# One decoder kernel: a norm between statistics and second softmax, sums behind the former norm, a reordered head, and semaphores cleared without a barrier

## The chip, the cores and the metric

The kernel runs on one core of a Trainium2 chip. The metric is the device time of one execution in microseconds (us). The core has five engines that run their own instruction queues in order and meet through semaphores: PE (TensorE, matrix products; its weight loads are listed as PEld), DVE (VectorE), ACT (ScalarE), POOL (GpSimd) and SP (SyncE, which here only issues DMAs).

## The reference, cut to what matters

The reference is a two-layer decoder over 64 sequences of 64 rows with 128 numbers each, all in float32. Six blocks follow one another, each added to the residual `x`:

```
x = x + L0_attn(layernorm(x))            # linear attention and a soft mixture of 4 experts
x = x + L0_xattn(ctx, layernorm(x))      # latent attention
x = x + L0_ffn(layernorm(x))             # shared MLP and 2 of 8 routed experts
x = x + L1_attn(layernorm(x))            # causal attention, below
x = x + L1_xattn(layernorm(x), ctx, mask)# attention with a relative bias
x = x + L1_ffn(layernorm(x))             # top expert of 8

# L1_attn, 16 heads of 8 numbers
q, k, v = heads(x @ Wq + bq), heads(x @ Wk + bk), heads(x @ Wv + bv)
att = softmax(where(causal, q @ k.T / sqrt(8), -inf))
y = (att @ v) @ Wo + bo
```

The change touches the border between the second and the third block, and the fourth block, the causal attention.

## The kernel before, in words

The whole residual `X` (32 tiles of 128 rows by 128) stays in SBUF. The six blocks are stages in one program: linear attention, latent attention, routing with the shared MLP (`route_and_share`), the routed experts (`run_experts`), causal attention (`causal_attention`), biased attention, top expert. Each stage is one block of code for each engine, and a barrier of all engines stands at the end of every block: an engine that is through waits until the last one is. Nothing but this barrier and the semaphores orders the engines. The order on each engine is written out by hand.

**The border of latent attention and routing.** Semaphores are scarce, so `reuse_semaphores` (lines 59 to 63) lets GpSimd clear the ones of the first two stages (L61), frees them, and puts a second barrier of all engines (L63) behind the one of the block's end. Only then do the engines enter `route_and_share`. PE begins there with L1279, DVE with the statistics of the last two tiles (L142 and after), GpSimd with a memset (L1331) and a root (L155).

**Causal attention** works in 16 steps of two tiles (256 rows, 4 sequences). For step s the work goes through these hands:

- SP gathers the two expert results of each row (L1825). GpSimd weighs them, adds the pair and adds this to `X` (L2153, L2158, L2164: "the sums" of a step, function `combine`).
- DVE takes the statistics of the rows (`norm_stats`, L142 to L149), GpSimd the inverse root (`norm_root`, L155), DVE applies the norm and writes `ca_xn` (`norm_apply`, L162).
- PE transposes `ca_xn` (L1901), ACT copies it out as `ca_hT` (L2058), PE projects q and k (L1909), ACT spreads them (L2063 and L2068), PE computes masked scores in two halves (L1933 adds the mask, L1938 the products).
- For each half DVE takes the maximum (L2231) and subtracts it (L2234), ACT takes the exponential (L2089), PE transposes (L1948), ACT copies (L2084), PE multiplies with v and the ones (L1965). DVE takes the reciprocal and the product of the step (`normalise`, L2239 and L2241), PE projects (L1977, L1979), DVE adds to `X` (`add`, L2246).

The steps are interleaved by `run_steps`, LEAD 3 and DEPTH 4: bodies 0, 1 and 2 are written out, 3 to 10 run in a loop of two bodies, 11 to 16 are written out again. Body s on DVE does, in order: first softmax of step s, statistics of step s+2, `add` of step s-2, second softmax of step s, norm of step s+2, `normalise` of step s-1. (Bodies 0 and 1 have their norm ahead of the second softmax.) Body s on PE does: first scores of s, transposes of the second half of s-1, `project` of s-2, the other transposes of s-1 and its first products, q and k projections of s+1 (between them a wait for the first softmax of s), second scores of s, v projection, transposes of the first half of s, the second products of s-1, then a wait for the second softmax of s, and last `turn_rows` of step s+2 (L1901), which waits for the norm of s+2.

GpSimd does, step after step, the sums and the root; for steps 1 to 3 it waits for the norm of the step before ahead of its sums, and for later steps it does not.

**The head of the stage** (before body 0) also computes keys and values of the next stage's first step: on PE `next_context`, four `next_keys` (L1851), `turn_rows` and `project_qk` of step 0, then `next_values` 4 and 5 (L1870, two passes for each); values 6 and 7 follow in body 0. ACT copies each of them (L2093).

**Late in the stage** SP waits for the sums of step 15 and then stores the relative bias in 254 KB of short rows and loads it back (L1831, L1836).

## Time and profile before

| | us |
|---|---|
| median of 3 runs (1894.44 to 1898.54) | 1895.55 |
| the profiled execution: its time | 1896.96 |
| the profiled execution: its span, first to last instruction | 1894.8 |
| PE busy | 1811.2 (96% of the span) |
| DVE busy | 1241.3 (66%) |
| ACT busy | 883.9 (47%) |
| POOL busy | 630.0 (33%) |
| mean granted clock of PE, 1 is full speed | 0.990 |

The stages stand at these places: linear attention to 414 us, latent attention to 955, routing and shared MLP to 1136, experts to 1247, causal attention to 1451, biased attention to about 1827, top expert to the end. The profiled execution took 1.41 us more than the median of the runs, and 2.16 us of its time lie outside its span. The page also gives the clock that PE was granted; it is at full speed nearly everywhere and at half in a few stretches of some us.

### The profile page before, as it was taken

Reading aid. Unit: us, or ns where it says so; the run is one execution under the profiler, and the core shown is the slowest. Engines: PE = TensorE matmul, PEld = TensorE weight load, DVE = VectorE, ACT = ScalarE, POOL = GpSimd, SP = SyncE. Lnnn points to the kernel's source line nnn. Section 1 sums busy time; section 2 is a strip of 40 time slices with the busy share of each in tenths; the row PEclk is TensorE's granted clock in tenths of the full one; section 3 lists DMA queues with packets and bytes.
Section 4 is the critical chain, followed back from the end, with each engine's and each line's share of the span. In section 5 each row is a group of like instructions: output and inputs, shape, how many; then the busy total and the mean of one; then the engine's idle time right before and its main releaser. Section 6 shows DMA issues by size and latency. Waiting matters only on the chain. (4 is left out here: it accounts for less than half of the span.)

```text
span 1894.8 us, 49825 instructions
## 1 busy us (share of the span) xinstructions
PE 1811.2 (96%) x20072; PEld 1353.8 (71%) x20072; DVE 1241.3 (66%) x2986; ACT 883.9 (47%) x1694; POOL 630.0 (33%) x744
## 2 busy tenths in 40 slices
PE   7999999999999999999999999989988999999978
PEld 5566666667888888888756667857766788888743
DVE  6677777647667766666643322237877888888877
ACT  1444444455555555555432213347664444445435
POOL 2111111113333333333314533342221444444547
PEclk9999999999999999999999999989999999999999
DMA  9200000000000000000010002210010000000001
GB/s 326 82 2 0 0 0 0 1 1 1 1 1 0 0 0 0 0 0 0 1 78 28 29 23 94 96 54 25 28 36 3 2 3 2 3 2 3 2 7 40
DMA packets 37926, 46.16 MB, mean 24 GB/s; under 512 B 5000, under 2 KB 32443, under 8 KB 37266
## 3 DMA queue, kind: packets, MB, share of 16 engines
q1 hardware_dynamic: 34450, 38.43, 6.5%
q0 software_dynamic: 3328, 5.58, 0.9%
q8 instruction: 115, 1.88, 0.4%
q14 instruction: 33, 0.27, 0.0%
HBM read 28.67 MB, written 17.10 MB: 24 GB/s over the span
## 5 line engine op out<-in xcount | busy, mean ns | idle before, releaser
L155 POOL TENSOR_TENSOR rstd<-var_eps,minus_half 128x2 f32<-128x2 f32 (+1 forms) x116 | 92.1, 794 | 466.6 <-DVE var_eps L149 466.4
L1069 POOL TENSOR_TENSOR xa_probs<-xa_probs,xa_total 128x512 f32<-128x512 f32 x128 | 133.0, 1039 | 196.4 <-DVE xa_total L1110 191.7
L1115 DVE TENSOR_REDUCE xa_top<-ps 128x4 f32<-128x512 f32 x128 | 88.1, 688 | 128.0 <-PE ps L934 126.7
L1030 ACT ACTIVATE xa_probs<-xa_probs 128x512 f32<-128x512 f32 x128 | 80.8, 631 | 157.4 <-DVE xa_probs L1118 157.4
L923 PEld LDWEIGHTS ps<-xa_kvT,pack_latent 128*128 128x128 f32 x512 | 96.6, 190 | 65.7 <-issue 43.7
L934 PE MATMUL ps<-xa_kvT,xa_qT 128*128 128x128 f32 x1024 | 135.3, 275 | 0.0
L950 PE MATMUL ps<-xa_probsT,xa_kv 128*128 128x512 f32 x256 | 133.2, 602 | 1.9 <-ACT xa_attnT L1039 1.8
L396 PEld LDWEIGHTS ps<-pack_moe,la_hid 128*128 128x128 f32 x1024 | 121.0, 192 | 17.4 <-issue 15.3
L383 PE MATMUL ps<-la_h2T,pack_moe 128*128 128x512 f32 x256 | 128.3, 609 | 3.9 <-ACT la_hid L592 3.9
L923 PE MATMUL ps<-xa_kvT,pack_latent 128*128 128x256 f32 x512 | 130.6, 380 | 1.4 <-PEq L344 1.4
L396 PE MATMUL ps<-pack_moe,la_hid 128*128 128x128 f32 x1024 | 125.2, 277 | 0.0
L934 PEld LDWEIGHTS ps<-xa_kvT,xa_qT 128*128 128x128 f32 x1024 | 124.5, 192 | 0.1
L592 ACT ACTIVATE la_hid<-ps,pack_moe 128x512 f32<-128x512 f32 x128 | 86.9, 686 | 80.2 <-PE ps L383 78.4
L958 PEld LDWEIGHTS ps<-pack_latent,xa_attnT 128*128 128x128 f32 x1024 | 118.2, 192 | 3.3 <-issue 2.5
L958 PE MATMUL ps<-pack_latent,xa_attnT 128*128 128x128 f32 x1024 | 119.6, 275 | 0.8 <-ACT xa_attnT L1039 0.8
L2416 PE MATMUL ps<-ba_inT,pack_latent 128*64 128x128 f32 x1920 | 118.1, 277 | 1.2 <-DVEq L1813 1.2
L2597 POOL TENSOR_TENSOR ba_probs<-ba_probs,ba_bias 128x512 f32<-128x512 f32 x64 | 81.4, 1272 | 101.1 <-DVE ba_probs L2662 101.1
L1463 DVE TENSOR_TENSOR rt_mid<-ps,rt_silu 128x512 f32<-128x512 f32 x64 | 44.2, 691 | 106.6 <-ACT rt_silu L1317 106.6
L1027 ACT ACTIVATE xa_probsT<-ps 128x512 f32<-128x512 f32 x128 | 76.8, 600 | 75.5 <-PE ps L943 75.5
L2416 PEld LDWEIGHTS ps<-ba_inT,pack_latent 128*64 128x64 f32 x1920 | 103.7, 137 | 8.0 <-issue 1.4
L1108 DVE TENSOR_REDUCE xa_total<-xa_probs 128x4 f32<-128x512 f32 x128 | 87.3, 682 | 22.2 <-ACT xa_probs L1030 21.6
L1118 DVE TENSOR_TENSOR xa_probs<-ps,xa_top 128x512 f32<-128x512 f32 x128 | 88.6, 692 | 13.0
(357 smaller groups left out, 4034.5 us busy)
## 6 DMA issues: line engine op xcount, KB each, us to landing
expert_weights<-experts_dram SPq DMA_DIRECT2D x8, 768.0 KB, 5.3
result_pairs<-zeros SPq DMA_DIRECT2D x1, 4096.0 KB, 30.9
ca_got<-result_pairs SPq DMA_DIRECT2D x16, 256.0 KB, 2.6
slot_rows<-zeros SPq DMA_DIRECT2D x1, 2880.0 KB, 19.7
expert_rows<-slot_rows SPq DMA_DIRECT2D x8, 360.0 KB, 3.1
pack_moe<-moe_dram SPq DMA_DIRECT2D x1, 2312.0 KB
pack_latent<-latent_dram SPq DMA_DIRECT2D x1, 2050.0 KB, 14.1
pack_latent<-biased_dram SPq DMA_DIRECT2D x1, 2048.0 KB, 8.0
```

What stands on the lines that cost most here:

```text
L155: pool.tensor_tensor(m.rstd[:, 0:tiles], m.var_eps[:, 0:tiles], m.minus_half[:, 0:tiles], ALU.pow).then_inc(sem.rstd, 1)
L383: pe.matmul(HIDDEN[n % 2], w["w1"][:, n // F0, n % F0, :], h2T[:], start=True, stop=True)\
L396: mm = pe.matmul(out, hid[:, n % 2, f, P * t:P * t + P], w["w2"][:, n, f, :], start=(f == 0), stop=(f == F0 - 1))
L923: mm = pe.matmul(bank(PROJ_BANK + n % 2)[:, NS * a:NS * a + NS], qk_fold[:, 2 * n + a, :], kvT[:, k, :, SEQ:], start=True, stop=True)
L934: mm = pe.matmul(bank(u % 2)[:, KEYS * n:KEYS * n + KEYS], qT[:, k, seq, head:head + 2, :].rearrange("p a q -> p (a q)"), kvT[:, k, seq, : ...
L950: pe.matmul(bank(ATTN_BANK), kv[:, k, seq, :], probsT[:, u % 2, :], start=True, stop=True)\
L958: mm = pe.matmul(bank(OUT_BANK)[:, P * t:P * t + P], attnT[:, t, h, :], vo_fold[:, h, :], start=(h == 0), stop=(h == H - 1))
L1069: pool.tensor_tensor(probs[:, u % 4], probs[:, u % 4], over(total[:, u % 4], 2, KEYS), ALU.mult).then_inc(probs_ready, 1)
L1108: dve.tensor_reduce(total[:, u % 4], probs[:, u % 4], AX.X, ALU.add).then_inc(sum_ready, 1)
L1115: dve.tensor_reduce(top[:, s % 4], scores, AX.X, ALU.max).then_inc(top_ready, 1)
L1118: dve.tensor_tensor(probs[:, s % 4], scores, over(top[:, s % 4], 2, KEYS), ALU.subtract)\
L2416: mm = pe.matmul(proj_bank(n)[SEQ * seq:SEQ * seq + SEQ, P * h:P * h + P], (w["bq"], w["bk"])[n // 4][:, at:at + DHX], tokens[:, seq], sta ...
```

## The change

In four parts:

1. `reuse_semaphores` is gone. The list of old semaphores is handed down (`past_semaphores`), the new stage takes fresh ones, and GpSimd clears the old ones at the start of `route_and_share`, between the barrier at the end of latent attention and its own first instruction. No second barrier follows.
2. On DVE the norm of step s+2 moves from behind the second softmax of step s to ahead of it, behind `add`, for bodies 2 to 13. Body 1 keeps its order (its norm stood ahead already). In body 0 the order is now softmax, statistics of step 2, softmax, norm of step 2, statistics of step 3; before, the statistics of step 2 stood ahead of the first softmax and the norm between the two.
3. On GpSimd the sums of every step from 4 on wait for the norm of the step before. The sums of step 3 are done right behind those of step 2, ahead of the root of step 2.
4. In the head, PE does `next_values(4)` ahead of `turn_rows` of step 0, ACT copies it ahead of the step's own copies, and ACT copies the context for the keys one instruction earlier (0.27 us between the two starts before).

```diff
-def reuse_semaphores(nc, m):
-
-    nc.clear_and_free_semaphores(m.stage_semaphores)
-    m.stage_semaphores = []
-    nc.all_engine_barrier()
+def past_semaphores(m):
+
+    past, m.stage_semaphores = m.stage_semaphores, []
+    return past
...
+        nc.clear_and_free_semaphores(past)
         with nc.Block() as block:
...
                 for n in range(4):
                     next_keys(n)
+                next_values(4)
                 turn_rows(step_of(0, 0), 0)
                 project_qk(step_of(0, 0), 0, None)
-                next_values(4)
                 next_values(5)
...
+                act.wait_ge(ctx_turned, 1)
+                act.activation(biased.inT[:, 1, :], bank(QK_BANK)[:, 0:NS], ACT.Copy).then_inc(ctx_ready, 1)
                 act.wait_ge(out_bias_done, 1)
                 act.wait_ge(zeroed, 2)
                 act.activation(tiles_of(out_bias[0:1, :]), over(bank(1)[0:1, 0:D], 1, 2), ACT.Copy).then_inc(out_bias_ready, 1)
-                act.wait_ge(ctx_turned, 1)
-                act.activation(biased.inT[:, 1, :], bank(QK_BANK)[:, 0:NS], ACT.Copy).then_inc(ctx_ready, 1)
                 for n in range(4):
                     copy_next_kv(n)
+                copy_next_kv(4)
                 rows(step_of(0, 0), 0)
                 copies_q(step_of(0, 0), 0)
                 copies_k(step_of(0, 0), 0)
-                copy_next_kv(4)
                 copy_next_kv(5)
...
-                for step in range(STEPS):
-                    if 1 <= step <= SETS:
-                        pool.wait_ge(ln.normed, 2 * step)
+                for step in range(2):
+                    combine(step)
+                    root(step)
+                    pool.wait_ge(ln.normed, 2 * step + 2)
+                combine(2)
+                combine(3)
+                root(2)
+                root(3)
+                for step in range(4, STEPS):
+                    pool.wait_ge(ln.normed, 2 * step)
                     combine(step)
                     root(step)
...
                         softmax(step, 0)
                     if ahead >= 2 and has(step, 2):
                         stats(later(step, 2))
-                    if ahead >= 2 and not has(step, 2):
-                        normed(later(step, 2))
+                    if not before:
+                        stats(later(step, 2))
                     if ahead == 0:
                         scale_mask()
                     if has(step, 2):
                         add(later(step, -2))
+                    if ahead >= 2 and before:
+                        normed(later(step, 2))
                     if here:
                         softmax(step, 1)
                     if not before:
+                        normed(later(step, 2))
                         stats(later(step, 3))
-                    if ahead >= 2 and has(step, 2):
-                        normed(later(step, 2))
...
-                stats(step_of(0, 2))
                 run_steps(dve, STEPS, body, DEPTH, LEAD)
...
-        reuse_semaphores(nc, m)
-        routed_experts(nc, m)
+        routed_experts(nc, m, past_semaphores(m))
```

What stands where is easiest seen in the order of the instructions. DVE in body 2, from `add` of step 0 on (`ca_top` and `ca_probs` are the second softmax of step 2, `ca_xn` the norm of step 4, `ca_rden` and `ca_attnT` belong to `normalise`), before:

```order
L2246 TENSOR_TENSOR X<-ps,X 128x256
L2231 TENSOR_REDUCE ca_top<-ps 128x16
L2234 TENSOR_TENSOR ca_probs<-ps,ca_top 128x1024
L162 TENSOR_SCALAR ca_xn<-X,mean_var,rstd 128x128 x2
L2239 RECIPROCAL ca_rden<-ps 128x256
L2241 TENSOR_TENSOR ca_attnT<-ps,ca_rden 128x256
```

The same place on DVE in the changed kernel:

```order
L2253 TENSOR_TENSOR X<-ps,X 128x256
L161 TENSOR_SCALAR ca_xn<-X,mean_var,rstd 128x128 x2
L2238 TENSOR_REDUCE ca_top<-ps 128x16
L2241 TENSOR_TENSOR ca_probs<-ps,ca_top 128x1024
L2246 RECIPROCAL ca_rden<-ps 128x256
L2248 TENSOR_TENSOR ca_attnT<-ps,ca_rden 128x256
```

The norm has moved from behind the second softmax to ahead of it; the reciprocal now follows the softmax at once.

POOL from the root of step 1 on to the root of step 3 (`ca_got` and `X` are the sums), before:

```order
L155 TENSOR_TENSOR rstd<-var_eps,minus_half 128x2
L2153 TENSOR_TENSOR ca_got<-ca_got,pair_weights 128x512
L2158 TENSOR_TENSOR ca_got<-ca_got 128x2x128
L2164 TENSOR_TENSOR X<-X,ca_got 128x256
L155 TENSOR_TENSOR rstd<-var_eps,minus_half 128x2
L2153 TENSOR_TENSOR ca_got<-ca_got,pair_weights 128x512
L2158 TENSOR_TENSOR ca_got<-ca_got 128x2x128
L2164 TENSOR_TENSOR X<-X,ca_got 128x256
L155 TENSOR_TENSOR rstd<-var_eps,minus_half 128x2
```

The same place on POOL in the changed kernel, behind the root of step 1:

```order
L2153 TENSOR_TENSOR ca_got<-ca_got,pair_weights 128x512
L2158 TENSOR_TENSOR ca_got<-ca_got 128x2x128
L2164 TENSOR_TENSOR X<-X,ca_got 128x256
L2153 TENSOR_TENSOR ca_got<-ca_got,pair_weights 128x512
L2158 TENSOR_TENSOR ca_got<-ca_got 128x2x128
L2164 TENSOR_TENSOR X<-X,ca_got 128x256
L154 TENSOR_TENSOR rstd<-var_eps,minus_half 128x2 x2
```

The sums of step 3 stand ahead of the root of step 2. The order of the later steps is as before; what is new there is the wait ahead of the sums.

PE in the head of the stage, from the keys on to the first scores (`ca_xn` and `ca_hT` belong to step 0; `pack_latent` with `ba_inT` are `next_values`), before:

```order
L1851 MATMUL ps<-ba_inT,pack_latent 64x128 x32
L1901 MATMUL ps<-pack_constants,ca_xn 128x128 x2
L1909 MATMUL ps<-ca_hT,pack_causal 128x256 x2
L1870 MATMUL ps<-pack_latent,ba_inT 128x512 x2
L1933 MATMUL ps<-pack_later_constants,pack_constants 32x256 x16
```

The same place on PE in the changed kernel:

```order
L1851 MATMUL ps<-ba_inT,pack_latent 64x128 x32
L1870 MATMUL ps<-pack_latent,ba_inT 128x512
L1901 MATMUL ps<-pack_constants,ca_xn 128x128 x2
L1909 MATMUL ps<-ca_hT,pack_causal 128x256 x2
L1870 MATMUL ps<-pack_latent,ba_inT 128x512
L1933 MATMUL ps<-pack_later_constants,pack_constants 32x256 x16
```

One of the two value products now stands ahead of the transposes of step 0.

## Rows read from the trace of the kernel before

**Rows 1.** Waits, 1290 to 1400 us: who waited for whom, us in total, times, longest.

```profile
DVE ca_top L2231 <- PE ps L1938: 15.0, 11, 1.6
...
PE ps L1901 <- DVE ca_xn L162: 4.5, 10, 0.6
```

**Rows 2.** Waits of PE, 1400 to 1430 us.

```profile
PE ps L1901 <- DVE ca_xn L162: 0.6, 1, 0.6
```

**Rows 3.** Timeline of one loop step: start, length, engine, work, [idle before <- releaser].

```profile
1325.44 1.23 DVE L2231 TENSOR_REDUCE ca_top<-ps 128x16 f32<-128x1024 f32 x1 [1.25 <-PE ps L1938]
...
1327.91 0.60 DVE L162 TENSOR_SCALAR ca_xn<-X,mean_var,rstd 128x128 f32 x2
...
1328.42 1.75 DVE L2239 RECIPROCAL ca_rden<-ps 128x256 f32<-128x256 f32 x1
...
1328.64 0.43 PE L1901 MATMUL ps<-pack_constants,ca_xn 128*128 128x128 f32 x2 [0.43 <-DVE ca_xn L162]
1328.74 1.05 ACT L2089 ACTIVATE ca_probs<-ca_probs 128x1024 f32<-128x1024 f32 x1
...
1330.32 0.66 PE L1948 MATMUL ps<-pack_constants,ca_probs 128*128 128x128 f32 x4
1330.55 1.21 DVE L2231 TENSOR_REDUCE ca_top<-ps 128x16 f32<-128x1024 f32 x1
...
1334.05 0.71 POOL L155 TENSOR_TENSOR rstd<-var_eps,minus_half 128x2 f32<-128x2 f32 x1 [6.92 <-DVE var_eps L149]
...
1334.73 1.05 POOL L2153 TENSOR_TENSOR ca_got<-ca_got,pair_weights 128x512 f32<-128x512 f32 x1
...
1335.80 1.23 DVE L2231 TENSOR_REDUCE ca_top<-ps 128x16 f32<-128x1024 f32 x1 [1.32 <-PE ps L1938]
...
1336.67 0.73 POOL L2164 TENSOR_TENSOR X<-X,ca_got 128x256 f32<-128x256 f32 x1
```

**Rows 4.** Timeline of DVE, second softmax of step 1 and of step 2.

```profile
1284.26 1.23 DVE L2231 TENSOR_REDUCE ca_top<-ps 128x16 f32<-128x1024 f32 x1 [3.19 <-PE ps L1938]
...
1294.20 1.22 DVE L2231 TENSOR_REDUCE ca_top<-ps 128x16 f32<-128x1024 f32 x1 [1.60 <-PE ps L1938]
```

**Rows 5.** Timeline, end of latent attention and start of routing: two barriers between.

```profile
954.62 0.42 DVE L1123 TENSOR_TENSOR X<-ps,X 128x256 f32<-128x256 f32 x1 [11.07 <-PE ps L958]
...
956.64 1.10 PE L1279 MATMUL ps<-turned_rows,pack_shared 128*128 128x512 f32 x2 [2.05 <-PEq L63]
```

**Rows 6.** Timeline, end of routing and start of the experts: one barrier between.

```profile
1134.85 0.69 DVE L1469 TENSOR_TENSOR X<-ps,X 128x512 f32<-128x512 f32 x1 [7.50 <-PE ps L1289]
...
1136.08 0.73 PE L1579 MATMUL ps<-pack_constants,expert_rows 128*128 128x128 f32 x5 [1.26 <-PEq L1226]
```

**Rows 7.** Waits of SP's queue, 940 to 965 us.

```profile
SPq L63 <- PEq L63: 1.0, 1, 1.0
```

**Rows 8.** Timeline of the causal stage's head.

```profile
1260.48 0.69 PE L1901 MATMUL ps<-pack_constants,ca_xn 128*128 128x128 f32 x2 [2.79 <-DVE ca_xn L162]
...
1263.51 3.60 PE L1870 MATMUL ps<-pack_latent,ba_inT 128*128 128x512 f32 x4
...
1264.66 1.02 ACT L2068 ACTIVATE ca_kpairs<-ps,ca_kbias,pack_constants 128x256 f32<-128x256 f32 x2
...
1267.03 0.71 PE L1933 MATMUL ps<-pack_later_constants,pack_constants 32*32 32x256 f32 x32
...
1268.35 1.98 PE L1870 MATMUL ps<-pack_latent,ba_inT 128*128 128x512 f32 x4
```

**Rows 9.** Windows: stretch, length, busy us of PE, PEld, DVE, ACT, POOL, clock, DMA, GB/s.

```profile
1266.00:1268.00 2.00, 2.00 (x42) 0.56 (x44) 0.00 (x0) 0.77 (x2) 1.84 (x3) 0.76 0.00 0
```

**Rows 10.** Timeline of SP and PE late in the stage.

```profile
1399.84 5.46 SPq L1831 DMA_DIRECT2D skewed_bias<-ca_by_offset  x2
...
1413.03 1.33 SPq L1836 DMA_DIRECT2D bias_values<-skewed_bias  x2
...
1414.82 0.54 PE L1965 MATMUL ps<-ca_probsT,ca_vheads 128*32 128x64 f32 x11 [4.20 <-issue]
```

More of the change, by code:

```diff
@@ L1132, in _, with routed_experts @@
                 dve.wait_ge(noted, 2 * (STEPS - 1))
-def routed_experts(nc, m):
+def routed_experts(nc, m, past):
     with ExitStack() as ctx:
@@ L1143, in routed_experts @@
         m.expert_loaded = [stage_semaphore(nc, m, "expert_loaded_" + name) for name in ("even", "odd")]
-        route_and_share(nc, m)
+        route_and_share(nc, m, past)
         run_experts(nc, m)
@@ L1154, in load_weights, with route_and_share @@
         .then_inc(m.expert_loaded[k], 16)
-def route_and_share(nc, m):
+def route_and_share(nc, m, past):
     w = m.w
```

## The prediction

> **What bounds the kernel now.** The page says that PE is busy for 96% of the span, so I asked in each stretch that the change touches what PE still waits for. In the table of waits of the causal loop PE has one wait worth naming: its transposes of a step's rows (L1901) wait for the norm on DVE, 4.5 us in 10 times [rows 1]. An eleventh, 0.6 us, stands behind it [rows 2], just ahead of a stall of 4.2 us in the middle of PE's products (L1965) that is put down to "issue", PE's own instruction supply [rows 10]. DVE waits for PE in the same loop, 15.0 us in 11 times [rows 1]: neither engine is full, they wait for each other in turn, and what decides is the order on DVE. The timeline of one step shows it [rows 3]. The second softmax starts at 1325.44, and from there to 1335.80 is one step, 10.36 us. The norm comes behind it at 1327.91, PE takes it at 1328.64 after 0.43 us of idling. But the root that this norm needs was ready a whole half step earlier: in the step that follows, the root ends at 1334.05 + 0.71 = 1334.76, and then DVE idles until 1335.80 (1.32 us of idle time before the softmax). The norm stands on the wrong side of a hole.
>
> **The loop: the norm into the hole.** The norm is two instructions, 0.60 us together. Put behind the root it runs from about 1334.85 to 1335.45, and the softmax is not due before 1335.80: it is hidden by DVE's wait for the scores, with 0.35 us to spare. Behind the softmax the reciprocal moves up from 1328.42 to 1327.91, so the next first softmax can start at 1330.55 - 0.51 = 1330.04 instead of 1330.55; PE's scores, moved up by its own wait of 0.43, ask for it at about 1330.0. Both engines move by nearly the same, so the step should shrink by PE's wait. Eleven such waits are 4.5 + 0.6 = 5.1 us. **Minus 5.1.** One step of the old trace already looks like this: in body 1 the norm stood ahead of the second softmax, PE did not wait, and from its second softmax to the next one are 1294.20 - 1284.26 = 9.94 us [rows 4], 0.42 less than 10.36.
>
> What is late next is ACT. PE's transposes at 1330.32 need the exponential that runs from 1328.74 to 1329.79 [rows 3]; moved up by 0.43 they stand at 1329.89, 0.10 behind it. So 0.43 is nearly all that there is to have, and at worst some of it is lost.
>
> **The loop: the sums behind the norm.** GpSimd now waits for the norm before the sums of the next step. In the old step's times they start at about 1335.5 instead of 1334.73, 0.75 later, and end 0.75 later. Behind the waiting instruction stand the sums and the next root. The statistics that read the sums come most of a step later: GpSimd sat idle for 6.92 us ahead of its root [rows 3]. Cost on the path: nothing, with 6 us of cover. The gathers that wait for a slot are three steps ahead.
>
> On why the wait is there: in the trace the softmax's maximum takes 1.23 us with sums beside it and 1.21 without them [rows 3], so these two do not disturb each other; a norm beside sums is not in these rows. The Trainium skill (SBUF — State Buffer, "Who interferes with whom") says that a tensor_scalar from SBUF to SBUF can need the port pair that DVE shares with GpSimd, and that the second to come is blocked for a whole instruction of the other. By that rule sums let go straight behind the root would hold the norm in the hole. The wait excludes this, so the sum above is the same with the rule and without it; the rule only gives the slow rival below its mechanism.
>
> **The late sums' other customer.** SP stores the relative bias when the sums of step 15 are done. These also come 0.75 us later against PE. The store was issued at 1399.84, the load that waits for its landing at 1413.03 [rows 10], and PE's stall, from 1410.6 on, ends at 1414.82, between 1 and 2 us behind that. I read the stall as PE's next piece of code being fetched behind the store's many short rows. If so, its end moves with the store: the stall grows by the same 0.75. Bounds: 0 (its end hangs on something else that moves with PE) and +0.75. I take the upper end, since the stall ends so near to the store's landing. **Plus 0.75.**
>
> **The border.** With two barriers PE starts 956.64 - (954.62 + 0.42) = 1.60 us after DVE's last instruction [rows 5]; at the next border, with one, it is 1136.08 - (1134.85 + 0.69) = 0.54 us [rows 6]. The difference is 1.06; SP's queue waits 1.0 us for the second barrier [rows 7]. The clearing itself stays on GpSimd alone. Its first result that anyone needs is the root behind DVE's statistics, about 1 us into the stage, so it has cover for that long, and any excess would delay only DVE's small norm, not PE's first products. Bounds 0.8 and 1.06. **Minus 1.0**, since the stage is PE-bound from its first instruction and everything behind moves up with it, the gathers included.
>
> **The head.** PE idles 2.79 us for the norm of step 0 (L1901 at 1260.48), and later does four passes of two value products at 1263.51 in 3.60 us, ahead of the first scores at 1267.03 [rows 8]. One product now falls into the idle time, which costs nothing there, and 1.8 us go from in front of the scores. But the scores also need ACT's spread keys, ready at 1264.66 + 1.02 = 1265.68. So they start at about 1265.74, 1.29 earlier. Of this some goes again: those four passes took 3.60 us where the same four took 1.98 a little later [rows 8], because PE's clock is at half speed there until about 1267 (mean 0.76 over the window from 1266 [rows 9]). Scores that start earlier run in the slow stretch: the 1.32 us from 1267.03 to 1268.35 become up to twice as long until 1267, so the values behind them start at about 1267.5 instead of 1268.35. Bounds 0 (DVE or ACT next late) and 1.29; I take 0.8. DVE's new order in body 0 has the first softmax no longer behind statistics, so it can follow. **Minus 0.8.** The keys that start 0.27 earlier end in the idle time: nothing.
>
> **The sum.** -1.0 - 5.1 + 0.75 - 0.8 = -6.15 us. The profiled execution, 1896.96, would become 1890.8, with a span of 1888.65; it lies 1.41 above the median of the runs. From the median: 1895.55 - 6.15 = **1889.4 us**, 0.32% faster.
>
> **The rivals.**
> A. The clock stays up in the head. PE idled 2.79 us and found half speed; with a value product in it the idle time is about 1.9, and the fall may not come. Then the chain from 1260.48 to the scores runs at full speed: the four passes show 1.98 against 3.60 [rows 8], and at this rate the two projections save 0.9 too. The scores come at about 1264.5 and the values behind them at 1265.8, 2.55 earlier than before instead of 0.8: 1887.7. For it: the idle time is shorter. Against it: still the longest of the head. The Trainium skill (TensorE: Matmul & The Clock Gate, "What's actually happening") says that the monitor runs free of the kernel, so by it this could differ from run to run; no run here shows that yet.
> B. The DVE wait goes and another takes half of its place, ACT's exponential first of all (0.10 of cover). Then the loop gives 2.5 instead of 5.1: 1892.0. Against it: the 9.94 of body 1. For it: body 1 has no statistics and no `add`.
> C. The store gets out of the way: if PE's fetch is asked for before the store begins, 0.75 later is enough to let it pass, and the 4.2 us go, with the 0.75. 1889.4 - 4.95 = 1884.5. For this the fetch would have to be asked for within that 0.75 us, of a step of some 10.
> D. Slower: the sums come ahead of the norm on the shared port, or the wait holds the wrong side. The three sums last 1336.67 + 0.73 - 1334.73 = 2.67 us [rows 3]. A norm behind them ends at about 1337.5 + 0.6 = 1338.1 instead of 1335.45; with 0.35 of cover the second softmax is 2.3 late in every step: 9.93 + 2.3 = 12.2 against 10.36, 1.9 us in each of 11 steps, +21 instead of -5.1: about 1915. It decides from 0.35 + 0.43 = 0.78 us of delay of the norm on. Against it: the norm needs the root alone, and the wait keeps the sums behind it.
> That the change doesn't do what it says is excluded: the order of the instructions shows all four parts.
>
> **How the numbers follow.** Chances: the forecast 0.52 (1887.5 to 1891), A 0.17, B 0.17, C 0.06, D 0.04, and 0.04 for a mean clock that is worse elsewhere by one or two slow stretches (up to 3 us, 1892.5). A measurement of this kernel can tell about 0.2%, 3.8 us, from no change: faster is below 1891.8. The forecast, A, C and nearly half of B are faster (0.81 together, 0.78 with the spread of the runs, which is 4 us); the rest of B and the bad clock are the same, 0.17; slower 0.05. The range runs from 1886.5 (A and its spread) to 1892.5 (B), which leaves out C, D and the tails.
>
> **What would show each step.** No wait of L1901 for `ca_xn` in the loop, and a step of about 9.93 from second softmax to second softmax; the norm in DVE's hole, 0.1 behind the root; the stall at L1965 near 4.95 with the store's issue 0.75 nearer to it; 0.5 to 0.8 us between DVE's last instruction and PE's first at the border; one value product in PE's idle time and the first scores 1.3 earlier against the norm of step 0. The prediction is wrong if the step stays above 10.1, if the stall changes by more than 1 us, or if the stage behind takes back what this one gives.

## The result, and the profile after

| | before | after |
|---|---|---|
| median of 4 runs each, us | 1897.05 | 1885.68 |
| lowest to highest | 1894.44 to 1898.68 | 1881.68 to 1886.33 |
| profiled execution, span | 1894.8 | 1884.4 |

The ratio is 0.9943, with a 95% interval of 0.992 to 0.9965. The forecast was 1889.4 us, with a range of 1886.5 to 1892.5: the direction was right, and the time lies below the range. Two more measurements of the changed kernel, in later groups of runs, gave 0.9965 [0.9943, 0.9987] and 0.9951 [0.993, 0.9971]. The plain mean of the three is 0.9953, some 8.9 us. The median of the kernel before was itself 1893.4 to 1896.9 us in the larger groups (11 to 31 runs each), so the starting point of the forecast, 1895.55 from 3 runs, was only good to 2 us.

Read one profile against the other, stretch by stretch. The border first, in the timeline of the changed kernel (start, length, engine, work, idle time before and its releaser):

```profile
954.80 0.42 DVE L1122 TENSOR_TENSOR X<-ps,X 128x256 f32<-128x256 f32 x1 [11.07 <-PE ps L957]
...
955.76 1.10 PE L1279 MATMUL ps<-turned_rows,pack_shared 128*128 128x512 f32 x2 [1.00 <-PEq L896]
...
956.53 0.12 POOL L1331 MEMSET rt_half_power<- 128x32 f32 x1 [6.37 <-remote]
...
956.82 0.70 POOL L154 TENSOR_TENSOR rstd<-var_eps,minus_half 128x2 f32<-128x2 f32 x1 [0.16 <-DVE var_eps L148]
```

From DVE's last instruction to PE's first are now 955.76 - 955.22 = 0.54 us, against 1.60 in [rows 5]: 1.06 us less, as at the other border [rows 6]. The clearing holds GpSimd back to 956.53, 0.77 us behind PE's first product, and its root follows DVE's statistics by 0.16 us.

The loop, with the same two views as [rows 1] and [rows 3]. The waits, 1290 to 1400 us (PE has none left in this view):

```profile
DVE ca_top L2238 <- PE ps L1938: 5.3, 12, 0.5
DVE ca_xn L161 <- POOL rstd L154: 4.9, 11, 0.6
```

One step of the timeline:

```profile
1324.98 1.23 DVE L2238 TENSOR_REDUCE ca_top<-ps 128x16 f32<-128x1024 f32 x1 [0.46 <-PE ps L1938]
...
1327.75 0.43 PE L1901 MATMUL ps<-pack_constants,ca_xn 128*128 128x128 f32 x2
...
1333.08 0.71 POOL L154 TENSOR_TENSOR rstd<-var_eps,minus_half 128x2 f32<-128x2 f32 x1 [5.81 <-DVE var_eps L148]
...
1333.82 0.60 DVE L161 TENSOR_SCALAR ca_xn<-X,mean_var,rstd 128x128 f32 x2 [0.44 <-POOL rstd L154]
...
1334.50 1.05 POOL L2153 TENSOR_TENSOR ca_got<-ca_got,pair_weights 128x512 f32<-128x512 f32 x1 [0.72 <-DVE ca_xn L161]
...
1334.91 1.23 DVE L2238 TENSOR_REDUCE ca_top<-ps 128x16 f32<-128x1024 f32 x1 [0.49 <-PE ps L1938]
```

The norm stands in DVE's hole, 0.03 us behind the root. It is done 0.49 us before the softmax, the sums start 0.08 us behind it, and PE's transposes at 1327.75 wait for nothing. The step is 9.93 us, and PE has no gap in it.

The end of the stage is the place where the two profiles differ most. The marks are the second softmax of step 12 and the first of step 15. (The rows stored and loaded back in between are two stores of 254 KB each.) Before:

```profile
1398.30 1.23 DVE L2231 TENSOR_REDUCE ca_top<-ps 128x16 f32<-128x1024 f32 x1 [1.64 <-PE ps L1938]
...
1432.55 1.22 DVE L2231 TENSOR_REDUCE ca_top<-ps 128x16 f32<-128x1024 f32 x1
```

After:

```profile
1395.10 1.23 DVE L2238 TENSOR_REDUCE ca_top<-ps 128x16 f32<-128x1024 f32 x1 [0.43 <-PE ps L1938]
...
1397.52 4.88 SPq L1831 DMA_DIRECT2D skewed_bias<-ca_by_offset  x2
...
1410.86 1.33 SPq L1836 DMA_DIRECT2D bias_values<-skewed_bias  x2
...
1422.01 1.22 DVE L2238 TENSOR_REDUCE ca_top<-ps 128x16 f32<-128x1024 f32 x1
```

The stretch takes 34.25 us before and 26.91 after. PE's stall of 4.20 us [rows 10] is gone, and with it a stretch at half speed behind it. In windows (length, busy us of PE, PEld, DVE, ACT, POOL, clock, DMA share, GB/s), before from 1415:

```profile
1415.00:1420.00 5.00, 5.00 (x85) 3.46 (x82) 2.49 (x3) 1.81 (x3) 0.00 (x0) 0.50 0.68 197
```

and the changed kernel from 1405 to 1418, where the stores' rows and then the loads run:

```profile
1405.00:1418.00 13.00, 13.00 (x373) 9.97 (x388) 10.13 (x12) 9.55 (x23) 0.00 (x0) 1.00 0.46 105
```

The head is the last of the four parts. The changed kernel:

```profile
1262.68 0.44 PE L1901 MATMUL ps<-pack_constants,ca_xn 128*128 128x128 f32 x2 [3.04 <-DVE ca_xn L161]
...
1267.78 0.73 PE L1933 MATMUL ps<-pack_later_constants,pack_constants 32*32 32x256 f32 x32 [0.77 <-ACT ca_kpairs L2068]
...
1294.95 1.22 DVE L2238 TENSOR_REDUCE ca_top<-ps 128x16 f32<-128x1024 f32 x1 [0.43 <-PE ps L1938]
```

From PE's first transposes (L1901) to the second softmax of step 2 are 32.27 us, against 1294.20 - 1260.48 = 33.72 in [rows 4, 8]. Summed over the profile: up to the second softmax of step 2 +0.75 us (border and head gained, and a slow stretch at the start of the experts took more: mean clock 0.79 from 1134 to 1142, where it was 1.00 before); from there to the second softmax of step 12 100.15 instead of 104.10, -3.95; from there to the first of step 15 -7.34; behind it nothing more. That is 10.5 us, and 7.3 of it in a stretch that took 34. The pair is a favourable one: the same stretch took 33.2 to 34.3 us in the other profiles with a stall of 4.2 us or a little less, and 27.8 and 28.0 in two more profiles of the changed kernel.

### The profile page after: what moved, and what is told of

Its sections match the earlier page's. It is cut to its first block and busy times, and to the rows that moved or that the text cites. A ratio compares the mean times of both kernels' runs of the same rounds, so it can differ in the third digit from the quotient of the medians.

```text
span 1884.4 us, 49825 instructions
## 1 busy us (share of the span) xinstructions
PE 1810.4 (96%) x20072; PEld 1351.4 (72%) x20072; DVE 1241.9 (66%) x2986; ACT 884.4 (47%) x1694; POOL 631.5 (34%) x744
```

## The experiments

Three questions: is the loop's gain what the forecast says, what does GpSimd's wait do, and is the stall, which the forecast let grow by 0.75 us, where the extra gain is from. All ratios are to the kernel before, in the same group of runs.

**The two kernels again.** No edit.

> The kernel before, unchanged, for a second trace. Theory 1 (PE's stall of 4.2 us late in the causal stage is a piece of PE's code that queues behind the store of the relative bias, at a place set by the kernel): the stall is there again, 3.5 to 5 us, at the same matmul line, and the half-speed stretch behind it too. Theory 2 (the stall is an accident of one execution): it is absent or elsewhere. The expert stage, first copy of turned rows to the causal stage's first copy, took 113.6 us in the old trace and 116.8 in the new one: if that is an accident of the execution, it may come out anywhere between here.

One run, 1897.79 us; the stall 3.94 us, and the waits of L1901 as before.

> The changed kernel, unchanged, for a second trace and its ratio on this chip: 0.992 to 0.9965. Theory 1: no stall of PE above 1 us inside the last written-out bodies, again. Theory 2: the stall may be back. Loop step 9.95 to 10.05 us.

0.9965 [0.9943, 0.9987], span 1884.4. The loop is the same to 0.1 us, and PE's stall is 0.63:

```profile
1407.46 0.36 PE L1965 MATMUL ps<-ca_probsT,ca_vheads 128*32 128x64 f32 x10 [0.63 <-issue]
```

**The parts alone.** The border (the clearing on GpSimd, no barrier):

```
-        reuse_semaphores(nc, m)
-        routed_experts(nc, m)
+        routed_experts(nc, m, past_semaphores(m))
```

> The kernel before with the clearing moved into the stage and no second barrier, nothing else. From the rows of the border: minus 1.06 us, ratio 0.9994, the stall of 4.2 us unchanged. If the clearing moves more than the border (fresh semaphores, shifted code), the stall or the expert stage differs.

0.9986 [0.9971, 1.0001]. Its profile repeats the 0.53 us between DVE and PE; a gain of 1 us is inside the interval, and no more can be said. The stall (4.19) and the expert stage are as before.

The head (value product 4 and its copy ahead of the projections, the context copied first; the edit on PE is shown):

```
+                next_values(4)
                 turn_rows(step_of(0, 0), 0)
                 project_qk(step_of(0, 0), 0, None)
-                next_values(4)
```

> The kernel before with the reordered head alone: value product 4 ahead of the transposes of step 0, context copied first. My own sum said 1.3 us less from the norm of step 0 to the first scores, of which 0.8 stays up to the later steps; full speed of PE in that stretch would give up to 2.5. In the changed kernel 1.45 us (first trace) and 0.3 us (second trace) came out from norm 0 to the second softmax of step 2, with the statistics moved as well. Rival: the statistics of step 2 ahead of the first softmax hold it, so the head alone gives less than 0.5.

0.9998 [0.9984, 1.0013]. Its profile, from the first transposes on:

```profile
1262.59 0.44 PE L1901 MATMUL ps<-pack_constants,ca_xn 128*128 128x128 f32 x2 [2.20 <-DVE ca_xn L162]
...
1266.75 0.73 PE L1933 MATMUL ps<-pack_later_constants,pack_constants 32*32 32x256 f32 x32 [1.26 <-ACT ca_kpairs L2068]
...
1273.97 0.70 PE L1909 MATMUL ps<-ca_hT,pack_causal 128*128 128x256 f32 x2 [2.27 <-DVE ca_probs L2234]
```

and its windows (columns as above, the clock third from the end):

```profile
1270.00:1275.00 5.00, 1.99 (x39) 0.85 (x37) 3.76 (x10) 3.20 (x5) 1.73 (x3) 1.00 0.17 52
1275.00:1280.00 5.00, 4.31 (x82) 3.08 (x56) 3.18 (x8) 3.11 (x10) 2.02 (x3) 0.66 0.20 56
```

The clock stays up from 1262 to 1269 (mean 1.00; 0.51 from 1260 to 1267 before), and the scores come 4.16 us behind the transposes instead of 6.55. Then PE waits 2.27 us for DVE, which in the old order has statistics ahead of its first softmax, and goes to half speed behind that. The second softmax of step 2 comes 35.00 us behind the transposes, not 33.72.

This can't be put down to the moved product. The unedited head shows the same in another execution, that of the kernel before with its stores early (below): scores 4.15 us behind the transposes, the clock up, and then

```profile
1275.89 0.70 PE L1910 MATMUL ps<-ca_hT,pack_causal 128*128 128x256 f32 x2 [2.25 <-DVE ca_probs L2235]
```

with its second softmax of step 2 at 34.92 us; the second trace of the kernel before has 34.96. In the twelve profiles with DVE's old order in body 0 this stretch takes 33.5 to 35.0 us (mean 34.2), and the first softmax of step 0 stands 8.8 to 8.9 us behind the transposes in all of them, whether the scores come at 4.2 or at 6.6. So the reorder alone shows no gain, and what the first steps wait for is DVE.

The loop (DVE's order and GpSimd's waits, border and head as before):

> The kernel before with the change's loop alone: DVE's order of norm, statistics and softmax, and GpSimd's waits; border and head as before. Theory (the loop gives what the forecast gave it, 4.5 to 5.1 us, in every execution, and the stall at L1965 weighs little in most timed ones): step 10.04 us, no wait of L1901 for ca_xn, 5 to 6 us off in the median, a ratio of 0.997. Rival (the stall is in every execution, so the loop part, which moves the stores, brings its 6 to 7 us too): 11 us or more off, a ratio of 0.994. If the extra 1.7 to 3.2 us of the expert stage in the profiles of the changed kernel come from the loop's code, the time from the stage's start to the causal stage is 115.3 us here too, and 113.6 us otherwise.

0.9958 [0.9938, 0.9977], in 6 runs. From the first transposes to the second softmax of step 2 are 1294.90 - 1262.35 = 32.55 us here. In the eight profiles with DVE's new order this stretch takes 31.3 to 33.5 us (mean 32.4), and the first softmax stands 5.6 to 6.8 us behind the transposes. So a gain of the head's size is there with DVE's new order in the first bodies alone, with PE idle for 3.49 us ahead of the transposes and no product moved.

The expert stage has the slow stretch at its start here too (0.79 from 1134 to 1142; 1.00 in the kernel with the border alone), as in the profile of the changed kernel. It stands in seven of the eight profiles with the new order and in none of the other twelve, and from the first expert product to the transposes of step 0 the eight take 125.3 to 127.5 us, the twelve 124.2 to 125.0. The difference of the means, 1.6 us, takes back nearly all of the 1.8 us that the stretch behind it gains. Why code that runs 120 us later should do this, no run tells.

**The norm in the hole without GpSimd's wait.** DVE's order alone, on the kernel before:

```
                     if has(step, 2):
                         add(later(step, -2))
+                    if ahead >= 2 and has(step, 2):
+                        normed(later(step, 2))
                     if here:
                         softmax(step, 1)
                     if not before:
                         stats(later(step, 3))
-                    if ahead >= 2 and has(step, 2):
-                        normed(later(step, 2))
```

(for the first two bodies the order stays as it was)

> The kernel before with the norm ahead of the second softmax from body 2 on, nothing else: GpSimd's sums start straight behind the root, beside the norm. Theory of the loop: PE's wait of 0.43 goes in 11 steps, minus 4.5 to 5.1 us there. If sums and norm disturb each other, the norm takes 1 us or more instead of 0.60 and the step stays at 10.3 or grows. Stall theory 1: the store's issue stays 1.5 us behind the second softmax of step 12 or comes earlier against it, so the stall of 4.2 us stays; if it goes, the shorter step alone is enough.

1.001 [0.9989, 1.0031]: no gain at all. The timeline:

```profile
1346.77 1.05 POOL L2153 TENSOR_TENSOR ca_got<-ca_got,pair_weights 128x512 f32<-128x512 f32 x1
...
1346.83 1.87 DVE L162 TENSOR_SCALAR ca_xn<-X,mean_var,rstd 128x128 f32 x2 [0.35 <-POOL rstd L155]
```

The sums start with the norm, and its two instructions take 1.87 us instead of 0.60. The ten steps from the second softmax of step 2 take 107.06 us, 2.96 more than before. The groups over the loop, this kernel and then the changed one (mean ns behind the busy time):

```profile
L162 DVE TENSOR_SCALAR ca_xn<-X,mean_var,rstd 128x128 f32 x16 | 15.0, 977 | 2.4 <-POOL rstd L155 2.3
```

```profile
L161 DVE TENSOR_SCALAR ca_xn<-X,mean_var,rstd 128x128 f32 x16 | 4.8, 344 | 3.1 <-POOL rstd L154 3.1
```

The same from the other side, the changed kernel without the waits of steps 4 to 15:

```
                 for step in range(4, STEPS):
-                    pool.wait_ge(ln.normed, 2 * step)
                     combine(step)
```

> The changed kernel without GpSimd's wait for the norm ahead of the sums of steps 4 to 15. Theory (the wait keeps norm and sums apart, and the two hold each other up): the second norm instruction grows from 0.34 to about 0.9 to 1.05 us, PE waits for ca_xn again (0.6 us or more a step), a step takes about 10.7 us instead of 10.04, and the stores are issued some 1.5 us earlier against PE, so that the stall of 4 us and the half-speed stretch come back: about 6 + 7 us more than the changed kernel, a ratio of about 1.001 to the kernel before. Rival (the wait is unneeded, norm and sums share nothing that matters): the step stays at 10.0, and only the stall decides: a ratio of 0.9945 to 0.998.

0.9996 [0.9975, 1.0018]. The norm takes 978 ns an instruction, the step is 10.7 us in the mean, and the stall is back (3.92 us). The wait is what makes the new order pay. The Trainium skill (SBUF — State Buffer, "Who interferes with whom") has the rule that a DVE instruction of this kind and GpSimd's exclude each other on a shared port pair; 344 ns against 977 beside sums agrees with it.

The wait on the old order, for the last sums alone and for all:

```
-                    if 1 <= step <= SETS:
+                    if 1 <= step <= SETS or step == STEPS - 1:
                         pool.wait_ge(ln.normed, 2 * step)
```

> The kernel before, but the sums of step 15 wait for the norm of step 14, which here stands behind the second softmax: the store is issued some 4 us later against PE. Theory 1: the stall is not as it was; either gone (the piece of code is through before the store's rows crowd the rings), minus 6 to 7 us, or moved to a later piece of code. Theory 3: 3.9 to 4.2 us at the same place.

1.0006 [0.9984, 1.0029].

> The kernel before with the change's wait on GpSimd alone: the sums of every step from 4 on behind the norm of the step ahead of it, DVE's order as it was. Theory: in the old order that norm stands behind the second softmax, so the sums start some 4.4 us later against PE but still have cover: the loop's step stays at 10.36 us, with the 11 waits of L1901; the stores are issued at about 5.9 us behind the second softmax of step 12, and the stall is as where only the last sums wait, about 6.1 us: a ratio of 1.000 to 1.002. Rival (late sums hold up DVE's statistics, so GpSimd's wait is not free): the step grows by 0.2 us or more, over 2 us in all.

1.0004 [0.9988, 1.002]; the waits of L1901 stay and the step stays at 10.4. Late sums cost nothing in the loop, and the wait alone gains nothing: order and wait pay only together. In both the stores are issued 5.9 us behind the second softmax of step 12, and the stall is 6.12 us:

```profile
1406.57 1.57 SPq L1831 DMA_DIRECT2D skewed_bias<-ca_by_offset  x2
...
1419.12 0.54 PE L1965 MATMUL ps<-ca_probsT,ca_vheads 128*32 128x64 f32 x11 [6.12 <-issue]
```

**The stores and the stall.** The stores moved into the loop, ahead of step 9's gather:

```
+                    if step == 9:
+                        sp.wait_ge(offsets_copied, 1)
+                        for par in range(2):
+                            sp.dma_start(m.skewed[par] ...).then_inc(offsets_stored, 16)
```

> The kernel before, with the two stores of the relative bias issued inside the loop, ahead of step 9's gather, when PE asks for no code, and nothing else changed. Theory (PE's stall of 4.2 us at L1965 is its code queued behind the stores' 508-byte rows, and the half-speed stretch behind it comes from that idling): the stall is under 0.3 us, the granted clock is 1.0 from 1410 to 1425, and the second half of that stage is 6 to 7.5 us shorter; the median falls by about 6.8 us, a ratio of 0.9965. Rival (the stall hangs on the old order of DVE's norm, since it was also absent in the changed kernel): the stall stays at about 4.2 us and the ratio is 1.000.

> The kernel before with the stores issued inside the loop, once more, with 5 rounds. Theory (the stall of the profile is not in ordinary executions): a ratio of 1.000. Rival (it is, and the first 10 runs were slow by chance): a ratio of 0.9965.

The profile does what the theory asks. The marks of the stage's end:

```profile
1403.55 1.22 DVE L2232 TENSOR_REDUCE ca_top<-ps 128x16 f32<-128x1024 f32 x1 [1.64 <-PE ps L1939]
...
1431.56 1.21 DVE L2232 TENSOR_REDUCE ca_top<-ps 128x16 f32<-128x1024 f32 x1
```

```profile
1415.00:1428.00 13.00, 12.45 (x374) 9.10 (x372) 10.09 (x17) 9.35 (x22) 0.00 (x0) 1.00 0.02 4
```

(the second is the window 1415 to 1428.) 28.01 us instead of 34.25, in both executions: stall and slow stretch together are 6.24 us against that profile (5.2 to 5.3 against three others of the old loop, whose slow stretch is shorter), and both come from the stores. But the ratios are 1.0001 [0.9985, 1.0016] in 10 runs and 1.000 [0.9984, 1.0017] in 12, where 0.9965 was expected. The median does not show what the profile shows.

The same edit on the changed kernel:

> The changed kernel, but SP issues the store ahead of the gather of step 9, in the middle of the loop, where PE runs code that it has. Theory 1: no stall of PE anywhere near the loop's end, and none in the loop either; against the changed kernel the same or up to 0.6 us less (the small stall of one of its traces). If the store's rows disturbed PE by themselves and not its code, a wait would show in the loop. The gathers behind the store land up to 13 us later and have three steps of cover, 30 us.

> The changed kernel with the stores issued inside the loop, once more, with 5 rounds. Against the kernel before with its stores early it has the change without the stall in either. Theory: the difference of the two is the forecast's sum without its term for the stall, 6.9 us, with half a microsecond to two more that the spread allows: a ratio to the kernel before of 0.9955 to 0.9965. Rival (something beyond loop, border and head gives the rest): 0.994 or less.

0.9941 [0.9922, 0.996] and 0.9949 [0.993, 0.9969]: with the stores out of the way in both kernels the change is worth as much as with them in place. Early against early, the medians lie 8.4 us apart (in two groups of runs) and 9.9 (in one). The second ratio fits neither what was expected of it (0.9955 to 0.9965) nor its rival (0.994 or less). The stage's end is 26.9 us as in the changed kernel.

The stall put back into the changed kernel (GpSimd doesn't wait ahead of the last sums, so that the stores go out at 0.9 us behind the second softmax of step 12 instead of 2.4):

```
-                    pool.wait_ge(ln.normed, 2 * step)
+                    if step < STEPS - 1:
+                        pool.wait_ge(ln.normed, 2 * step)
```

> The changed kernel, but the sums of step 15 alone don't wait for the norm of step 14, so the store of the relative bias is issued 0.6 to 0.9 us earlier against PE, about 1.5 us behind the second softmax of step 12, as before the change. Theory 1 (PE's stall depends on when the store starts against PE's code fetches): the stall of about 4 us and the half-speed stretch behind it are back, plus 6 to 7 us on the new trace. Theory 3 (the shorter loop step or the shifted code did away with it, the store's start has nothing to do with it): no stall above 1 us, and no change beyond the norm of step 14 being held for about 1 us. The loop steps before are 10.0 us either way.

```profile
1411.88 0.47 PE L1965 MATMUL ps<-ca_probsT,ca_vheads 128*32 128x64 f32 x10 [3.90 <-issue]
```

0.9963 [0.9947, 0.998], against 0.9953 for the mean of the changed kernel's three. The profile lost 5.5 us at the stage's end against the first profile of the changed kernel (4.6 against the second), the median hardly any.

The stores 1.37 us later on the kernel before:

```
                 sp.wait_ge(combined, STEPS * ADDS)
+                sp.wait_ge(ln.normed, 2 * (STEPS - 2) + 1)
```

> The kernel before, with SP waiting for the first half of the norm of step 14 ahead of the same two stores, which issues them about 1.3 us later against PE (2.85 us behind the second softmax of step 12 instead of 1.54), and nothing else changed. Theory (the code that PE asks for 8.2 us behind that softmax is let through between the first store and the second if the first is then still running): the fetch comes at about 9.4 to 10.5 us instead of 14.05, the stall shrinks from 4.2 to under 1.5 us, and the half-speed stretch goes; 4 to 7 us off, a ratio of 0.9965 to 0.998. The forecast's reading as it stood (the stall's end moves with the stores): the stall grows to about 5.5 us, a ratio of 1.001.

1.001 [0.999, 1.003]. The theory on record falls, and the forecast's reading holds here: stores 1.37 us later, stall 1.37 us longer.

```profile
1406.72 1.56 SPq L1832 DMA_DIRECT2D skewed_bias<-ca_by_offset  x2
...
1421.71 0.54 PE L1966 MATMUL ps<-ca_probsT,ca_vheads 128*32 128x64 f32 x11 [5.57 <-issue]
```

Three times the rows (the two stores repeated into scratch memory):

> The kernel before with the two stores of the relative bias made three times back to back, twice into scratch memory that nobody reads: 33 us of 508-byte rows instead of 11. Its loads come 22 us later, 20 us ahead of the stage that reads them. Theory (a code fetch of PE waits behind such rows in every execution): the profiled stall is 4.2 us or, where the fetch is let through at the end of the whole train only, up to 26 us, and the median moves as the profiled stall does: with a stall of 26 us a ratio of 1.011 or more. Rival (only the profiled execution waits there, the timed ones hardly do): the profiled span grows by what the stall grows, up to 22 us, and the median of the others stays within 3 us of the kernel before, a ratio of about 1.000.

0.9997 [0.9977, 1.0016], stall 4.20 us. The stores that follow don't hold the fetch up, so this magnified nothing. One long store ahead of the two did:

```
+                sp.dma_start(m.skewed_long ..., over(by_offset[:, 0:OFFSETS], 1, 4 * SEQ))
                 for par in range(2):
                     sp.dma_start(m.skewed[par] ...).then_inc(offsets_stored, 16)
```

> The kernel before with one more store ahead of the two of the relative bias, four times as long as one of them, into scratch memory that nobody reads: 33 us of 508-byte rows, the first 22 of them in one transfer. The loads that wait for the real ones come 22 us later, about 20 us ahead of the stage that reads them. It magnifies PE's stall. In the profile PE's code, asked for about 8 us behind the second softmax of step 12 at the latest, should come only near the end of the long transfer or later, and the stall grow from 4.2 to between 12 and 26 us. Theory (ordinary executions hardly have the stall): the median without the profiled run stays within 3 us of the kernel before, a ratio of 1.000. Rival (they all have it): the median grows by what the stall in the profile grows, at least 8 us, a ratio of 1.004 or more.

```profile
1421.59 0.54 PE L1967 MATMUL ps<-ca_probsT,ca_vheads 128*32 128x64 f32 x11 [8.60 <-issue]
```

1.0024 [1.0007, 1.004] in 12 runs: 4.5 us by the ratio (1.3 to 7.6 by the interval), where the stall grew by 4.4, not by the 8 or more that were expected. This one says that the timed executions have at least a part of this longer stall. It stands against the two with early stores, which show nothing of the shorter one.

The changed kernel a third time:

> The changed kernel itself, for a narrower interval beside the others. Theory (loop 4.5 to 5, border 1, head about 1 in every execution; the stall little): 6.5 to 7.5 us off, a ratio of 0.9962. Rival (the stall's 6 to 7 us come on top in every execution): 12 us or more off, a ratio of 0.9935.

0.9951 [0.993, 0.9971], span 1882.0, stall 0.80.

## Why the prediction was wrong

**The loop: the mechanism right, the size in part by luck.** With the stores early in both kernels, which leaves no stall in either, the stretch from the second softmax of step 12 to the first of step 15 is 28.01 before and 26.91 after, -1.10. With the -3.95 from step 2 to 12 the loop gives 5.05 us; forecast 5.1. But the ten waits of 4.5 us gave 3.95 and not 4.5: PE's steps now alternate between 9.93 and 10.15 (10.36 and 10.45 before), and in the longer ones PE still idles 0.12 us ahead of L1901, put down to "issue" and in the old order hidden in the wait. And there were twelve waits to win, not eleven. The twelfth can't be seen in the kernel before, where it stood behind the stall; with the stores early and the old order it shows:

```profile
PE ps L1902 <- DVE ca_xn L162: 1.1, 2, 0.6
```

(waits of PE, 1404 to 1430 us.) It made good what the ten were short of. ACT's exponential took nothing (rival B).

**GpSimd's wait: right, and worth more than the prediction said.** It said that the sum is the same with the rule on the shared port and without it. That is so; but the runs without the wait show that the whole of the loop's gain hangs on it. Rival D had the right mechanism and the wrong price: a norm beside sums takes 1.9 us, it is not held until all three are over, and the step grows to 10.7 us, not 12.2: both kernels without the wait came out level with the kernel before, not 21 us slower.

**The border: right**, 1.06 us in the profile, with the clearing hidden on GpSimd. The median can't tell 1 us.

**The head: the reason was wrong, and the sum isn't to be seen.** From the transposes on it is 1.45 us in this profile, 0.2 to 1.9 in three others of the change, forecast 0.8. The moved product alone showed nothing, although there the clock stayed up, as rival A has it: what bounds the first steps is DVE, and the forecast gave DVE's order half a sentence ("so it can follow"). With the longer expert stage ahead of it, the profiles with the new order win only 0.2 us in the mean from the first expert product to the second softmax of step 2. In the three profiles of the changed kernel PE still idled 2.3 to 3.0 us ahead of L1901, and its clock was 0.63 to 0.76 in the 7 us behind.

**The stall: this step failed.** The prediction took "the stall grows by the same 0.75" and -6.15 as the sum. In the profiled execution the stall went instead, and with it the slow stretch that the idle time had brought, 6.24 us in this pair. That was rival C, with 6 in 100, and its price of 4.95 lacked the slow stretch. What I had not seen is that the stall doesn't follow the stores in one way. With the stores at 0.9, 1.5, 2.9 and 5.9 us behind the softmax, in eleven profiles, it is 3.9 to 4.75, 3.9 to 4.2, 5.6 and 6.1 us. With them at 2.4 us, in four profiles (two kernels), it is 0 to 0.84. In all fifteen profiles with a stall of 0.6 us or more, PE goes on 2.2 to 2.5 us behind a packet of 16 KB on the queue of instructions; so the reading of the stall as code that comes late holds, and what failed is when it comes. The DMA view of the changed kernel, for the 1 us from 1404, 9 us behind the softmax (queue, packets, MB, share), has the rows of the stores (q1) and one packet of instructions (q8) among them:

```profile
q1 hardware_dynamic: 84, 0.04, 34.2%
q8 instruction: 1, 0.02, 5.5%
```

In the kernel before there is none from 1402 to 1412, and it comes at 1412, when the rows are over. But in the two with the stores at 5.9 us it comes at 16.0, some 2 us before the rows end, so "behind the last row" isn't the rule either. What lets it through at 2.4 us I can't say; the first guess, that it slips in between the two stores if it is asked for before the second, was refuted by the stores at 2.9 us.

**How much of the stall is in ordinary executions stays open.** Without the term for the stall the forecast's sum is -6.9 us, a ratio of 0.9964. The measured mean of 0.9953 has room for 2 us of the 6.24, give or take some 2.5 by the intervals, and hardly for all of it. Four comparisons bear on it. Stores early on the kernel before: 0 us, twice, where the profile gives 6.2. Stores early on both: the same ratio as with them in place. The stall put back: 2 us of 5.5, which is inside the noise. The long store: all of its 4.4. No one share of the stall in ordinary executions fits both the first and the last. The profiled executions themselves say that they are the special ones: in the twelve with a stall of 3.9 us or more, the profiled execution took 4.9 us more in the mean than the median of the other runs of its kernel (the single second trace taken against those of its group), and in the eight with less it took 1.0 us less. A reading that fits these, and that no run tests: ordinary executions have the stall, but shorter by some 4 us, which leaves nothing of 4.2 and about half of 8.6.

So the extra gain in the profile is explained, and that in the median is not. Part is the starting point (1895.55 from 3 runs, where the larger groups give 1893.4 to 1896.9; in the first comparison it was 1897.05, against which the ratio of 0.9943 is taken). The rest is 2 us, or 1.5 and 3 where the stores are early in both kernels, and lies about at the edge of what intervals of 0.2% can tell; which part of the change gives it stays open.

## What to carry to other kernels

Move an operation into another engine's idle hole only together with what keeps its neighbour off the shared port: here the order without the wait gave nothing, and both gave 5 us. Waits that are read in the order of one engine can be summed over their occurrences, but look for one more that a stall hides, and don't expect each to come back whole: here ten of 4.5 us gave 3.95. A stall at "issue" beside a train of short DMA rows is not a quantity that simply shifts with the rows: give it both ends, gone and grown. One profile against one other can't price a head of a stage whose length varies by 1.5 us from one execution to the next. And what one profiled execution gains in one place is not yet a gain of the median: take the cause away from the kernel before and time that.

## What the runs showed of the hardware

PE's instruction fetch can come some 10 us late beside other DMA traffic. With the rows out of the way the packets of instructions came 8.1 to 8.4 and 12.1 to 13.2 us behind the second softmax of step 12, and PE had no stall. With the two stores in the usual place the first came at 14.1, and PE stood for 4.20 us; with the long store it came at 18.4, 16 us behind the one before, and PE stood for 8.60 us.

Behind a stall of 4.2 us the granted clock is at half for some 7 us in two profiles (0.50 from 1415 to 1420), and for about half as long in two others (0.76 from 1414 to 1421 with the stores made three times). Against the 28.01 us without the stores the stretch grows by 6.24 us in the first and by 5.2 in the others.

DVE's tensor_scalar on 128x128 takes 344 ns alone and 977 beside GpSimd's tensor_tensor, which itself stays at 1.05 us.

The start of each stage varies from one execution to the next. PE's first product of routing started between 954.0 and 960.0 us in the twenty profiles, where the code ahead of it differs by one barrier, 1 us. Single profiles of this kernel are no measure of a few us.
